# Transformer block on one core: order of TensorE's products and PSUM banks in the self-attention loop, and banks and order in the cross-attention opening

## What is computed

```python
x = x + cross_attention(layernorm(x), ctx_1024)   # 16 heads of 64, 256 context rows a batch, layernorm behind it
x = x + self_attention(layernorm(x))              # 16 heads of 16, RoPE, softmax over 64 keys
x = x + moe(layernorm(x))                         # shared expert + top 2 of 8

# self-attention
q, k, v = x @ Wq.T + bq, x @ Wk.T + bk, x @ Wv.T + bv      # heads split off
q, k = rope(q), rope(k)
attn = softmax(q @ k.T * Hd ** -0.5)
return (attn @ v) @ Wo.T + bo
```

## Time and profile before

| | |
|---|---|
| runs | 2158.69, 2160.77, 2160.35 us |
| the profiled execution | 2161.38 us, of which the span from first to last instruction is 2159.6 us |
| PE / DVE / ACT / POOL busy | 97% / 73% / 59% / 44% of the span |
| stages, us of the span | cross-attention to about 1400, self-attention loop about 1400 to 1640, experts to the end |
| granted TensorE clock, mean | 0.991 of 2.4 GHz |

### The profile page before, as it was taken

How to read it: one execution, slowest core, us unless ns; L and a number is a source line. 1 busy time by engine, 2 the same in 40 slices (tenths; PEclk the granted TensorE clock), 3 DMA queues, 4 the chain that set the end, 5 groups by cost and what they waited for, 6 DMA issues and landing times.

```text
span 2159.6 us, 46904 instructions
## 1 busy us (share of the span) xinstructions
PE 2099.8 (97%) x15864; PEld 1853.6 (86%) x15865; DVE 1568.7 (73%) x2774; ACT 1269.5 (59%) x3067; POOL 941.1 (44%) x786
## 2 busy tenths in 40 slices
PE   7999999999999999999999999899998999999997
PEld 6889899888988898898998888678886888888886
DVE  5667767777677677677677776699996877666665
ACT  4656666665666666556666656467775335555553
POOL 3322332333233224223323332278884334777775
PEclk9999999999999999999999999999999999999999
DMA  5000010010000000100100100145442222333332
GB/s 154 6 25 22 13 34 19 15 34 15 19 24 24 19 24 10 34 22 12 34 19 15 34 10 1 48 157 167 156 129 94 88 79 55 56 53 53 53 54 42
DMA packets 100685, 103.90 MB, mean 48 GB/s; under 512 B 11952, under 2 KB 90160, under 8 KB 100624
## 3 DMA queue, kind: packets, MB, share of 16 engines
q1 hardware_dynamic: 86992, 84.47, 12.5%
q0 software_dynamic: 13632, 18.62, 5.4%
HBM read 72.52 MB, written 30.54 MB: 48 GB/s over the span
## 4 chain that ended last, share of the span: by engine, by line
PE 75%; POOL 9%; issue 6%; DVE 5%; ACT 2%; DMA 2%; POOLq 0%; SPq 0%; DVEq 0%; ACTq 0%
PE banks L930 38%; PE banks L973 6%; PE banks L1003 5%; PE banks L1031 5%; PE banks L1018 5%; POOL out_dram L2431 4%; PE banks L1672 3%; POOL r_x L2395 3%; PE banks L2270 2%; POOL index L2402 2%; DMA out_dram<-r_y,index 1%; PE banks L960 1%; PE banks L1735 1%; PE banks L1694 1%; PE banks L1751 1%
## 5 line engine op out<-in xcount | busy, mean ns | idle before, releaser
L930 PE MATMUL banks<-ctxT_hi,qk_hi 128*128 128x256 f32 x1024 | 301.5, 294 | 0.0
L930 PE MATMUL banks<-ctxT_hi,qk_lo 128*128 128x256 f32 x1024 | 290.1, 283 | 0.0
L930 PE MATMUL banks<-ctxT_lo,qk_hi 128*128 128x256 f32 x1024 | 288.2, 281 | 0.0
L562 ACT ACTIVATE probs<-banks,nbias 128x256 f32<-128x256 f32 x512 | 236.3, 486 | 81.1 <-DVE nbias L695 80.7
L451 POOL TENSOR_TENSOR rinv<-rsum,inverse 128x4 f32<-128x4 f32 x96 | 96.7, 1007 | 410.9 <-ACT probs L562 410.9
L569 ACT ACTIVATE pc<-banks 128x512 f32<-128x512 f32 x256 | 153.0, 598 | 190.4 <-PE banks L930 187.2
L653 DVE TENSOR_TENSOR qk_lo<-banks,qk_hi 128x512 fp32r<-128x512 f32 x256 | 163.7, 686 | 88.4 <-ACT qk_hi L524 88.3
L690 DVE TENSOR_REDUCE peak<-banks 128x4 f32<-128x1024 f32 x128 | 156.4, 1222 | 81.6 <-PE banks L930 81.6
L653 DVE TENSOR_TENSOR pT_lo<-banks,pT_hi 128x512 fp32r<-128x512 f32 x256 | 164.7, 685 | 58.2 <-ACT pT_hi L524 57.7
L930 PE MATMUL banks<-pT_hi,ctx_hi 128*128 128x512 f32 x512 | 204.7, 400 | 1.7 <-DVE pT_lo L653 1.7
L930 PE MATMUL banks<-pT_hi,ctx_lo 128*128 128x512 f32 x512 | 201.6, 394 | 0.0
(11 more groups left out here) (271 smaller groups left out, 6161.0 us busy)
## 6 DMA issues: line engine op xcount, KB each, us to landing
ctx_raw<-in_ctx_dram SPq DMA_DIRECT2D x64, 256.0 KB, 2.7
experts_w<-in_L_ffn_We_dram SPq DMA_DIRECT2D x24, 512.0 KB, 3.9
x_in<-in_x_dram SPq DMA_DIRECT2D x16, 256.0 KB, 2.8
x_again<-in_x_dram SPq DMA_DIRECT2D x16, 256.0 KB, 2.8
x_stream<-z SPq DMA_DIRECT2D x16, 256.0 KB, 2.1
s_x<-x_stream SPq DMA_DIRECT2D x32, 128.0 KB, 3.7
s_x_again<-x_stream SPq DMA_DIRECT2D x32, 128.0 KB, 3.2
x_normalised<-s_xl SPq DMA_DIRECT2D x32, 128.0 KB, 1.7
```

Of the source, the lines that this page charges most:

```text
L562: nc.scalar.activation(probs[:, s % 2, p, :], scores[:, s % 2, p // 2, (p % 2) * SK:(p % 2 + 1) * SK], ACT.Exp, bias=nbias[:, s % 2, p:p + ...
L930: last = nc.tensor.matmul(out, a, b, start=(n == 0), stop=(n == 3 * len(pairs) - 1))
```

## The change

In the self-attention step PE's order becomes xT, qkT, y, qk, scores, x3T, pT, gate, v, o: the turned queries ahead of the Wo product, and the next tile's values product ahead of the probabilities' product. Banks 1 and 3 are dealt out anew; bank 0 keeps xT, qk and o. The instruction lists of ACT, DVE, POOL and SyncE in this stage keep their order. In the opening (kind -1) the ring's keys take the four banks in turn; in group 0 `qbk0` goes ahead of the first `wk` on PE and DVE, `peaks` goes ahead of `wk_lower`, and `wk` alternates between banks 0 and 1; POOL does `weights_by_bk` once for each column half of Wq, starting when the first has landed.

```diff
@@ ring_order @@
+        if kind == 0 and s == 0:
+            out.append(("qbk0",))
         if kind == 0 and s < 2:
             out += [("wk", 2 * s), ("wk", 2 * s + 1)]
-        if kind == 0 and s == 0:
-            out.append(("qbk0",))
...
-SINGLE_BANKS = {"ctxT": (1, 2, 2, 2), "o": (3, 0), "wk": (0, 1, 2, 3), "xT": (3,), "qbk": (1,), "qbk0": (2,)}
+SINGLE_BANKS = {"ctxT": (1, 2, 2, 2), "o": (3, 0), "wk": (0, 1, 0, 1), "xT": (3,), "qbk": (1,), "qbk0": (3,)}
-def ring_bank(key):
+def ring_bank(key, kind):
+    if kind == -1:
+        return ring_order(kind).index(key) % RING
...
@@ gpsimd: weights_by_bk @@
-        def weights_by_bk(c):
-            nc.gpsimd.tensor_tensor(products[:, 0], wq_raw[:, c, :], biases[:, 0], ALU.mult).then_inc(wqb_step, 1)
+        def weights_by_bk(half, c):
+            done = WQB_STEPS * (DC * half + c)
+            cols = slice(half * HALF * DK, (half + 1) * HALF * DK)
+            nc.gpsimd.tensor_tensor(products[:, 0, cols], wq_raw[:, c, cols], biases[:, 0, cols],
+                                    ALU.mult).then_inc(wqb_step, 1)
...
-                pool.wait_ge(wq_in[0], 16)
-                pool.wait_ge(wq_in[1], 16)
                 pool.wait_ge(bk_in, 16)
-                for c in range(DC):
-                    weights_by_bk(c)
+                for half in range(2):
+                    pool.wait_ge(wq_in[half], 16)
+                    for c in range(DC):
+                        weights_by_bk(half, c)
...
@@ vector, group 0 @@
-                    for i in range(2):
-                        wk_lower(g, i)
                     dve.wait_ge(wqb_done, 1)
                     keep_qbk(g, ("qbk0",))
...
                 if g.cur:
                     peaks(g, s)
-                if g.kind == 0 and s == 1:
-                    for i in range(2, 4):
+                if g.kind == 0 and s < 2:
+                    for i in range(2 * s, 2 * s + 2):
                         wk_lower(g, i)
@@ tensor, group 0 @@
                 if g.cur:
                     do_scores(g, s)
+                if g.kind == 0 and s == 0:
+                    pe.wait_ge(wqb_done, 1)
+                    do_qbk(g, ("qbk0",))
                 if g.kind == 0 and s < 2:
                     for i in range(2 * s, 2 * s + 2):
                         do_wkT(g, i)
-                if g.kind == 0 and s == 0:
-                    pe.wait_ge(wqb_done, 1)
-                    do_qbk(g, ("qbk0",))
@@ pair_order (pe_step is moved in the same way) @@
         if g.has(s, 2):
             out.append(("xT", s))
+        if g.has(s, 1):
+            out.append(("qkT", s))
         if g.has(s, -2):
             out.append(("y", s))
-        if g.has(s, 1):
-            out.append(("qkT", s))
...
             out.append(("gate", s))
+        if g.has(s, 1):
+            out.append(("v", s))
         if g.has(s, -1):
             out.append(("o", s))
-        if g.has(s, 1):
-            out.append(("v", s))
...
-BANKS = (("xT", "qk", "o"), ("y", "pT0"), ("qkT", "x3T", "gate"), ("pT1", "v"))
+BANKS = (("xT", "qk", "o"), ("pT0", "v"), ("qkT", "x3T", "gate"), ("y", "pT1"))
```

More of the change, by code:

```diff
@@ L280, in cross_attention @@
     pool_past = sem("pool_past")
-    bank_turns = [Turns(lambda kind, k=k: [key for key in ring_order(kind) if ring_bank(key) == k], -1, GROUPS)
+    bank_turns = [Turns(lambda kind, k=k: [key for key in ring_order(kind) if ring_bank(key, kind) == k], -1, GROUPS)
                   for k in range(RING)]
@@ L289, in place @@
     def place(g, key, groups_on=0):
-        k = ring_bank(key)
+        k = ring_bank(key, g.at + groups_on if isinstance(g.at, int) else g.kind)
         if isinstance(g.at, int):
@@ L456, in normalise @@
                                     ALU.mult).then_inc(probs_pool, 1)
-        def weights_by_bk(c):
-            nc.gpsimd.tensor_tensor(products[:, 0], wq_raw[:, c, :], biases[:, 0], ALU.mult).then_inc(wqb_step, 1)
-            pool.wait_ge(wqb_step, WQB_STEPS * c + 1)
+        def weights_by_bk(half, c):
[3 more added lines that the diff above has]
+                                    ALU.mult).then_inc(wqb_step, 1)
+            pool.wait_ge(wqb_step, done + 1)
             n = DK // 2
-            parts = products[:, 0].rearrange("p (h d) -> p h d", d=DK)
+            parts = products[:, 0, cols].rearrange("p (h d) -> p h d", d=DK)
             for i in range(WQB_STEPS - 1):
-                out = parts[:, :, 0:n] if n > 1 else wqb[:, c, :].unsqueeze(2)
+                out = parts[:, :, 0:n] if n > 1 else wqb[:, c, half * HALF:(half + 1) * HALF].unsqueeze(2)
                 nc.gpsimd.tensor_tensor(out, parts[:, :, 0:n], parts[:, :, n:2 * n], ALU.add).then_inc(wqb_step, 1)
-                pool.wait_ge(wqb_step, WQB_STEPS * c + i + 2)
+                pool.wait_ge(wqb_step, done + i + 2)
                 n //= 2
@@ L472, in gpsimd @@
                 rsqrt(g, 0, ln_stats, ln_rstd, 1)
-                pool.wait_ge(wq_in[0], 16)
-                pool.wait_ge(wq_in[1], 16)
                 pool.wait_ge(bk_in, 16)
-                for c in range(DC):
-                    weights_by_bk(c)
+                for half in range(2):
+                    pool.wait_ge(wq_in[half], 16)
+                    for c in range(DC):
+                        weights_by_bk(half, c)
                 nc.gpsimd.tensor_copy(wqb_hi[:, :, :], wqb[:, 0:DC, :]).then_inc(wqb_step, 1)
-                pool.wait_ge(wqb_step, WQB_STEPS * DC + 1)
+                pool.wait_ge(wqb_step, WQB_STEPS * DC * 2 + 1)
                 nc.gpsimd.tensor_tensor(wqb_lo[:, :, :], wqb[:, 0:DC, :], wqb_hi[:, :, :],
@@ L1688, in pe_step @@
             last.then_inc(done, 1)
+        if g.has(s, 1):
+            pe.wait_ge(turn_done, g.tile(s, 2))
+            bank, done = bank_for(pe, g, ("qkT", s))
+            for c in range(4):
+                last = nc.tensor.transpose(bank[:, c * P:(c + 1) * P], spun[:, 0, c * P:(c + 1) * P], ident[:, :])
+            last.then_inc(done, 1)
         if g.has(s, -2):
@@ L1694, in pe_step @@
                 last = nc.tensor.matmul(bank[:, 0:D], oT[:, m, :], woT[:, m, :], start=False, stop=(m == DC - 1))
[L1695 to L1700, removed]
             last.then_inc(done, 1)
@@ L1743, in pe_step @@
             last.then_inc(done, 1)
+        if g.has(s, 1):
+            bank, done = bank_for(pe, g, ("v", s))
+            exact3(bank[:, 0:D], [((xT_hi[:, o, c, :], xT_lo[:, o, c, :]),
+                                   (w_hi[:, c, 2 * D:], w_lo[:, c, 2 * D:])) for c in range(DC)]
+                   ).then_inc(done, 1)
         if g.has(s, -1):
@@ L1755, in pe_step @@
             last.then_inc(done, 1)
[L1756 to L1761, removed]
     def tensor(pe):
```

## The result

The changed kernel takes 2164.84 us (median of 20 runs, 2159.59 to 2167.98) against 2160.91 for the kernel before (20 runs, 2157.67 to 2162.84): 1.0018 of its time, interval 1.0012 to 1.0025. It is 0.18% slower, 3.9 us, by two parts that nearly cancel. The forecast was 2169, range 2162 to 2178, slower.

The account below looks back on a forecast made before the run. PE sets the self-attention pace, DVE close behind; in the opening PE waits for banks. Against the profiled 2161.38, - 12.5 (opening) + 21.2 (loop) = + 8.7, so 2170.1; less 1.0 for the median, 2169 us, range 2162 to 2178.

Parts of the forecast that it names:

- The loop: Self-attention: xT must wait for ACT's oT copy, 0.72 us a step over 28 steps, 20.2; 21.2 with the last steps.
- 2.89 less 0.09: Self-attention step, gate's begin to next xT: 0.51 after gate, v 0.77, o and copy 1.61; 0.09 given back by v.
- rival (b): Loop and opening cancel: 0.45 us a step against 13 in the opening, busy PE hiding waits ahead of o; chance 0.08.
- The last steps: Two self-attention steps with v but no xT: y waits for oT, about 0.8 us in one, 0.2 in the other.
- The opening: Scores 7.7 us earlier, first turned probabilities another 5.3 or 3.4 sooner; 12.5 us gain taken, bounds 10 to 14.
- POOL's sums: Opening: sums in column halves end at about 26, qbk0 wants them at 29.5; hidden with 3 us of cover.
- the better of my two cases: Opening at full clock: folds 0.61 us apart, scores 7.7 us earlier, then 5.3 saved, 13.0 in all.
- the worse case: Opening's folds at half clock, 0.9 us apart instead of 0.61 from fold 3 on: some 1 us less gain.
- y and qkT: Self-attention swap of y and qkT costs and gives nothing; without xT's stall, qkT would wait about 0.3 us a step.
- (c): Faster: in self-attention v fills PE's wait for pT copies; decides from 0.43 us a step downwards, about 2157; chance 0.12.
- (d): Opening gains only 4 to 8 us, from late Wo, late POOL sums or half clock: 2173 to 2178; chance 0.13.
- (e): PE's new idling drops its clock inside the self-attention loop; three half-clock steps give 2187; chance 0.05.

Follow-up runs that it names:

- e1: Only the self-attention part of the change, opening and cross-attention as in the kernel before: 2179.94 us, 1.0083 of that kernel's time.
- e2: Only the opening's part of the change, self-attention as in the kernel before: 2146.54 us, 0.9927 of that kernel's time.
- e4: Kernel before with only qkT moved ahead of y in the self-attention loop, v still behind o: 2163.21 us, 1.0008.
- e7: The opening's part alone, but with POOL's sums undivided as before, against the kernel before: 2146.89 us, 0.9933.
- e11: The whole changed kernel timed and profiled once more, against the kernel before: 2163.70 us, 1.0011.
- e5: Self-attention part alone, with o moved from bank 0 to bank 3, opening as before: 2176.20 us, 1.0068 of the kernel before.

## Why the prediction was right, and where its sizes were off

**The loop: mechanism right, 20% too large.** The forecast was 0.72 us a step and 21.2 in all; measured 0.64 a step, 17.8 in the profile and 17.6 in e1. From gate's begin to the next xT it is 1495.83 - 1493.11 = 2.72, where I had 2.89 less 0.09. The term that was mis-sized is gate to v and o: v begins 0.41 behind gate, not 0.51; v takes 0.91 with its change to o, not 0.77; and o's begin to xT's begin is 1.40 us, not 1.61, because o takes 0.65 when it has no copy to wait for. I read 1.61 at the loop's end, where o still waited in its middle. So v's place gave back 0.17 us a step, not the 0.09 that the weight loads' idle time showed: the page's busy matmuls hid the rest, as rival (b) had it, though not by enough for (b).

**The last steps** were put at 1 us. From the last xT to the last oT copy it took 23.3 us before (1614.34 to 1637.60) and 23.8 after (1614.68 to 1638.47): 0.5.

**The opening: 12.5 forecast, 14.7 in the profiles, 15.8 in e2 (interval 13.0 to 18.8).** Between the end of the first ctxT_lo and the first turned probabilities it took 29.6 us before (21.0 to 50.64) and 17.2 after (18.83 to 35.98), which is 12.5 less. In all, the six profiles with the old opening have 29.5 to 30.5 there and the four with the new one 16.8 to 17.2: 12.9 us. So the total was right, but partly by two errors that cancel. Up to the scores' begin the gain was 8.6 us and not 7.7: they begin 4.7 us behind the first ctxT_lo, where I had 26.6 - 21.03 = 5.6, since PE transposed the three ctxT from 21.97 on, while the qk_lo still ran to 23.61. From there to the first turned probabilities it was 3.9 and not 5.3, since that took 12.4 us (23.54 to 35.98) and not 11.0: PE waited 0.58 for POOL's sums and 0.37 for DVE's normalising, and the scores took 3.1 each, not 2.89. The term that was mis-sized most is this one, and the wait for POOL's sums, put at nothing, is the largest part of it.

The rest of the 14.7, 2.2 us, lies ahead of that stretch and is no step of the change. The first Wk heads are turned from 8.39 us on in the profile before and from 7.57 on in the profile after, and their 32 transposes take 3.33 us in the one and 1.97 in the other. Nothing in the diff stands ahead of them, and kernels with the old code up to there can have both: in e4's profile, with the old opening, they start at 7.39 and take 1.97, and the first probabilities are turned at 48.44. Over all twelve profiles the start lies between 7.2 and 9.2 us and the 32 take 1.97 (four times) or 3.0 to 3.7 (eight times). All four with the whole new opening start by 7.7, but so do two of the other eight, so I take it for scatter of the runs; that is not shown.

**The clock** came out as in the better of my two cases in the first profile and in e2's: granted 1.00 while the folds ran. In e7's and e11's it was 0.58 and 0.57 between 20 and 24 us, as in the worse case, and scores began 5.5 and 5.6 us behind the first ctxT_lo instead of 4.7. The price of 0.8 to 0.9 us is near the "some 1 us" forecast. In these two PE had no wait for POOL, which made up for it: the whole stretch took 16.8 and 17.0 us.

**POOL's sums** were said to be hidden with 3 us of cover. They were not, quite: they ended at 27.20 and PE idled 0.58 us for them in the profile after and in e2's; in e11's and e7's profiles, where PE came to the scores 1.5 to 2.2 us later (at 25.70 and 25.77) and the sums ended at 26.31 and 26.25, there was no wait. My 3 us of cover also counted on scores that begin at 26.6, and they began at 23.54. I had 26 for the sums. A cast of 32 columns, 0.21 us in the other ten profiles, took 1.08 in these two, beside a 1024-column subtraction of DVE (wq_lo). And the splitting of ctx that follows the sums did count: DVE's normalising took 2.15 us beside it (33.78 to 35.93), where it took 1.22 and 1.23 in e7's and e11's profiles, with POOL already done. With 1.22 it would have ended at about 35.0, ahead of PE's own list (35.61), and the wait of 0.37 would not be there.

**y and qkT:** right beside v's move. Taken alone I expected 0.1 to 0.3 us a step and e4's profile shows 0.11. What I missed is that in the new order qkT stands close behind the logits copy too. In the changed kernel xT's stall covers that, so it cost nothing; it showed once the stall was gone (e5).

**The rivals.** (c), v filling a wait for pT's copies, exists at 0.17 us a step, less than half of the 0.43 from which it would have decided. (d) did not happen. (e) did not happen: with 0.75 us of idling in each 7.91 the clock stayed at 1.00 through the loop, so the rule of the Trainium skill ("TensorE: Matmul & The Clock Gate", psum-queue depth-cycling) did not show in this loop.

**What should be run** is the opening's part alone: 2146.5 us, 0.7% faster than before and 0.9% faster than the changed kernel (by 0.9927 against 1.0018). It can do without POOL's halves as far as the runs can tell.

## What to carry to other kernels

When a product is moved in a ring of few banks, ask what stood between each bank's last reader and its next writer: a product that seemed to be merely late may have been the cover for a copy. Follow every wait of the products behind it, the bank of the next one too: a copy in an in-order list holds up all that is freed behind it, and taking away one of two such waits gave back only 3 of 17.6 us. And time a change's parts apart before judging it: a measured 0.2% hid - 0.7% and + 0.8%.

## What was not expected of the hardware

The first turned Wk heads, with the same code ahead of them, started between 7.2 and 9.2 us after the span's start in twelve profiles, in five of them after a wait for the Wk load; and their 32 transposes took 2.0 us in some and up to 3.7 in others. In an opening this short that is as much scatter as an edit is worth. And GpSimd's 128x32 cast took 1.08 us instead of 0.21 in the two profiles in which DVE worked on 1024 columns beside it; in both it ended 0.07 us after that instruction (26.85 after 26.78, 27.51 after 27.44). So small GpSimd instructions on a critical chain can cost more than their usual row says.
